# Scores of the first attention pass as float32r products in two halves of the array, with products that nobody reads

## The chip, the core and the metric

The kernel runs on one core of a Trainium2 chip. The metric is the device time of one execution in microseconds. The engines of a core work side by side and wait for each other by semaphores: TensorE (PE in the rows; its weight loads are PEld), VectorE (DVE), ScalarE (ACT), GpSimd (POOL) and SyncE (SP, which issues the transfers here; SPq is its queue).

## What is computed

A vision transformer's layer on 128 images. The part that the change touches is the first attention, without a mask, over 197 tokens of 192 numbers in 12 heads of 16:

```python
x = (tokens - mean) / jnp.sqrt(var + LN_EPS) * ln_w + ln_b
xh = x.reshape(n, SEQ, N_HEADS, D_HEAD)
q = jnp.einsum('bshd,hed->bshe', xh, Wq) + bq[None, None]
k = jnp.einsum('bshd,hed->bshe', xh, Wk) + bk[None, None]
v = jnp.einsum('bshd,hed->bshe', xh, Wv) + bv[None, None]
att = jax.nn.softmax(jnp.einsum('bshd,bthd->bhst', q, k) / jnp.sqrt(jnp.float32(D_HEAD)), axis=-1)
msa = jnp.einsum('bhst,bthd->bshd', att, v).reshape(n, SEQ, HIDDEN_D)
return tokens + msa
```

Behind it come a second attention with a causal mask, a layer norm, a mixture of experts with soft routing, and another layer norm.

## The kernel before, in words

The program is five passes over the images, each with its own tiles and a barrier behind it: `embed_pass` (patches to tokens, norm, q, k and v of the first attention), `attend_pass(causal=False)` (tiles a_...), `attend_pass(causal=True)` (tiles c_...), routing with the experts (r_..., x_...) and `combine_pass` (o_...). Each pass is a pipeline written by hand: in step c, every engine works on several images, each at another stage. `pipeline` (L124) writes the first steps and the last out, and makes the middle a loop of R = 4 steps; in the first attention pass the steps 0 to 7 are written out, and the loop begins with step 8. In the loop an image's number is an expression of the loop's register, and `is_number(i)` (L84) is true only where the number is known when the program is built.

Scores need float32 accuracy. So `embed_pass` splits q and k into three bfloat16 parts: ScalarE the high part (L310), VectorE the remainder `rest` (L338), GpSimd the middle and low parts (L282, L284). SP stores them to `qk1`, three parts of two bytes. The first attention pass loads them stacked: 6 pairs of parts, each of 16 rows, give a contraction of 96 rows (`STACK`) in which one bfloat16 product has all that counts of q times k. Three more rows (`AUG`) carry the negated maxima of the scores in three parts against rows of ones.

One step of the first attention pass has six slots k = 0 to 5 on TensorE (L901 to L972). In each slot stand, for image b4, four key products (`key_scores`, L843, into the banks `sk`; they include the rows of the maxima, and ScalarE's exponential reads them, L713), and for image b2, four query products (`query_scores`, L821, two into each of the banks `sq`; VectorE takes their maxima, L770, which are all that is kept of them). A query product waits until VectorE has read the bank's content before. Then the slot's other work follows: in slot 0 the tokens are turned (L925, float32) and the value products of the last group (L858, float32, four column strips of 32) stand; in slot 1 the maxima are turned (L890) and the sums (L864); in slot 2 the q projection for the second attention (`turned_times`, L873, twelve float32r products) and value products; in slot 3 the sums are turned (L864); in slot 4 the k projection and value products; in slot 5 the v projection (L881, twelve float32r products). Between the q and the k projection ScalarE and VectorE split q (L726, L784). GpSimd splits the maxima (`max_parts`, four operations, L611 to L618), and SP writes their three rows into `qs` (L561).

The routing pass already has `keep_warm` (L1230): products of a tile of ones into a bank that nobody reads, one at three places of a step, and 24 at step 12.

Of the kernel before, what the change touches and what calls it, by code (L numbers as in the profile page):

```python
# [22 lines left out]
F32 = mybir.dt.float32  # L23
# [7 lines left out]
HEADS = 12  # L31
# [150 lines left out]
def embed_pass(nc, n, A, scr):  # L182
    R = 4
    DEPTH = 4
    with ExitStack() as ctx:
# [17 lines left out]
        rest = m.sb("e_rest", [CH, 2, 2, 2, SP])  # L203
        parts = m.sb("e_parts", [CH, R, 2, 2, PARTS, SP], BF16)
# [30 lines left out]
        middle = m.event("e_middle", 2)  # L235
        low = m.event("e_low", 2)
# [5 lines left out]
        def _(sp):  # L242
# [10 lines left out]
            def step(c):  # L253
# [4 lines left out]
                if b.inside(n):  # L258
                    sp.wait_ge(v_copied.sem, v_copied.at(b))
                    for rows in SHARES:  # L260
                        sp.dma_start(scr["tv1"][b.number, rows], tv[rows, b.place]).then_inc(stored.of(b), 16)
                    sp.wait_ge(low.sem, low.at(b))
                    sp.dma_start(scr["qk1"][b.number].rearrange("i c a p s -> p (i c a) s"),
                                 parts[:, b.place].rearrange("p i c a s -> p (i c a) s")).then_inc(stored.of(b), 16)
# [3 lines left out]

        @block.gpsimd
        def _(pool):  # L270
            for e in (middle, low):
                e.seed(pool)

            def step(c):
                b = c - 3
                u = b.parity
                if b.inside(n):
                    for i in range(2):
                        pool.wait_ge(left.sem, left.at(b, i + 1))
                        pool.wait_ge(stored.of(b - 4), stored.at(b - 4))  # L280
                        m.hold(pool)
                        pool.tensor_copy(parts[:, b.place, i, :, place_of(i, 1)], rest[:, u, i]).then_inc(middle.sem, 1)  # L282
                        pool.wait_ge(middle.sem, middle.at(b, i + 1))
                        pool.tensor_tensor(parts[:, b.place, i, :, place_of(i, 2)], rest[:, u, i], parts[:, b.place, i, :, place_of(i, 1)],  # L284
                                           ALU.subtract).then_inc(low.sem, 1)
            pipeline(pool, n, DEPTH, R, step)

        @block.scalar
        def _(act):
# [5 lines left out]
            def step(c):  # L295
# [11 lines left out]
                for i, (done, p) in enumerate(((q_done, qp), (k_done, kp))):  # L307
                    if b3.inside(n):
                        act.wait_ge(done.sem, done.at(b3))
                        split_high(nc.scalar, parts[:, b3.place, i, :, place_of(i, 0)], p[:], SCALES[i]).then_inc(high.sem, 1)  # L310
# [9 lines left out]
        def _(dve):  # L320
# [14 lines left out]
            def left_of(b3, i, p):  # L335
                dve.wait_ge(high.sem, high.at(b3, i + 1))
                dve.wait_ge(low.sem, low.at(b3 - 2, i + 1))
                nc.vector.scalar_tensor_tensor(out=rest[:, b3.parity, i], in0=p[:], scalar=SCALES[i],  # L338
                                               in1=parts[:, b3.place, i, :, place_of(i, 0)], op0=ALU.mult,
# [88 lines left out]
def attend_pass(nc, n, A, scr, causal):  # L428
# [4 lines left out]
    with ExitStack() as ctx:  # L433
        m = Memory(nc, ctx, R)
        qs = m.sb(X + "qs", [AUG, R, HEADS, SP], BF16)
        ks = m.sb(X + "ks", [AUG, R, HEADS, SP], BF16)
# [5 lines left out]
        mxp = m.sb(X + "mxp", [HEADS, 2, PARTS, SP], BF16)  # L442
# [18 lines left out]
        else:  # L461
            rest = m.sb(X + "rest", [CH, 2, SP])
            kf = m.sb(X + "kf", [CH, 2, SP])
# [22 lines left out]
        qk_in_place = m.transfers(X + "qk_in_place", 2 * PARTS)  # L486
# [9 lines left out]
        max_in_place = m.transfers(X + "max_in_place", 3)  # L496
# [33 lines left out]

        def heads_of(fill):
            return (fill % 2, 2 * (fill // 2)) if causal else (fill // 6, 2 * (fill % 6))

        @block.sync
        def _(sp):
# [7 lines left out]
            def step(c):  # L543
                b = c - 1
                if b.inside(n):
                    sp.wait_ge(scored_k.sem, scored_k.at(b - R))
                    at = 0
                    for a in range(PARTS):
                        rows = slice(at, at + (PARTS - a) * DH)
                        at = rows.stop  # L550
                        for i, (stack, of) in enumerate(((qs, slice(0, PARTS - a)), (ks, slice(a, PARTS)))):
# [1103 lines left out]
```

## Time and profile before

| | us |
|---|---|
| median of 3 runs (4807.69 to 4813.0) | 4812.62 |
| the profiled execution | 4837.32 |
| its span, first to last instruction | 4835.4 |

| engine | busy us | share of the span |
|---|---|---|
| TensorE products | 4495.4 | 93% |
| TensorE weight loads | 3885.2 | 80% |
| VectorE | 3048.0 | 63% |
| ScalarE | 2720.1 | 56% |
| GpSimd | 2701.4 | 56% |

The span's stages follow one another, so a share of the whole span tells little of a stage: the stretches have to be read by themselves. A product's recorded duration contains its way through the array; the pace of products is read from start to start. The granted clock of TensorE has two levels in the rows, 1.00 and 0.50 of 2.4 GHz.

### The profile page before, as it was taken

How to read it: one execution, taken by the hardware profiler on the slowest of the kernel's cores; microseconds unless marked ns; L12 is line 12 of the kernel's file. 1: busy time of each engine (PE TensorE's matmuls, PEld its weight loads, DVE VectorE, ACT ScalarE, POOL GpSimd, SP SyncE). 2: the span in 40 equal slices, each digit the busy share in tenths (PEclk: the TensorE clock that was granted, in tenths of full speed). 3: DMA queues.
4: the chain of work that ended last, by engine and by line, in shares of the span. 5: the costliest groups of instructions: out<-in, count | busy, mean ns of one | idle time of the engine just before them, and what ended most of it. 6: DMA issues, size and time to landing. Idle time of an engine off the chain costs nothing. (4 is left out here: it accounts for less than half of the span.)

```text
span 4835.4 us, 161306 instructions
## 1 busy us (share of the span) xinstructions
PE 4495.4 (93%) x48311; PEld 3885.2 (80%) x48311; DVE 3048.0 (63%) x8728; ACT 2720.1 (56%) x6788; POOL 2701.4 (56%) x4491
## 2 busy tenths in 40 slices
PE   8999999899999999999979999999999788889965
PEld 8999999688888888888868888888887566678853
DVE  4555555566666666666647777777776799930058
ACT  3444444466666666666635555555555477753346
POOL 3444444466666666666646666666666588841135
PEclk9999999899999999999979999999999799999965
DMA  6777777677777777777756666666664233369978
GB/s 170 202 202 202 203 202 201 151 166 165 168 168 167 168 166 168 165 165 167 169 110 141 145 142 145 142 146 143 146 141 111 76 93 93 93 156 247 241 233 258
DMA packets 697918, 789.88 MB, mean 163 GB/s; under 512 B 367345, under 2 KB 519887, under 8 KB 697840
## 3 DMA queue, kind: packets, MB, share of 16 engines
q1 hardware_dynamic: 697840, 788.92, 67.6%
q8 instruction: 40, 0.66, 0.1%
q14 instruction: 38, 0.31, 0.0%
HBM read 519.30 MB, written 265.72 MB: 162 GB/s over the span
## 5 line engine op out<-in xcount | busy, mean ns | idle before, releaser
L770 DVE TENSOR_REDUCE a_mx<-a_sq 99x2 f32<-99x394 f32 x1536 | 797.3, 560 | 378.5 <-PE a_sq L821 378.2
L770 DVE TENSOR_REDUCE c_mx<-c_sq 99x2 f32<-99x198 f32 (+1 forms) x1536 | 641.8, 458 | 255.9 <-PE c_sq L821 254.6
L713 ACT ACTIVATE a_ex<-a_sk 99x792 f32<-99x792 f32 (+1 forms) x768 | 638.1, 831 | 107.8 <-PE a_sk L843 57.3
L713 ACT ACTIVATE c_ex<-c_sk 99x792 f32<-99x792 f32 (+1 forms) x768 | 509.4, 663 | 208.2 <-PE c_sk L837 137.7
L379 PE MATMUL e_tokp<-e_wmap,e_ptT 128*99 128x192 f32 x3072 | 544.2, 327 | 20.8 <-DVE e_cvar L332 20.8
L379 PEld LDWEIGHTS e_tokp<-e_wmap,e_ptT 128*99 128x99 f32 x3072 | 483.2, 167 | 21.2 <-issue 20.8
L821 PE MATMUL a_sq<-a_ks,a_qs 96*99 96x198 bf16 x3072 | 441.1, 255 | 31.6 <-DMA a_ks<-scr_qk 16.6
L634 POOL TENSOR_SCALAR_AFFINE_SELECT c_ex<-c_ex 99x396 f32<-99x396 f32 (+1 forms) x768 | 408.0, 546 | 91.5 <-ACT c_ex L713 82.0
L282 POOL CAST e_parts<-e_rest 96x396 bf16<-96x396 f32 x256 | 176.4, 689 | 482.5 <-DVE e_rest L338 482.5
L821 PE MATMUL c_sq<-c_ks,c_qs 96*99 96x99 bf16 (+1 forms) x3072 | 424.8, 231 | 0.0
L843 PE MATMUL a_sk<-a_qs,a_ks 99*99 99x198 bf16 (+1 forms) x3072 | 408.7, 254 | 2.7 <-issue 2.1
L843 PEld LDWEIGHTS a_sk<-a_qs,a_ks 99*99 99x99 bf16 (+1 forms) x3072 | 287.5, 126 | 124.3 <-issue 112.9
L818 PE MATMUL c_sq<-c_maskb,c_identb 99*99 99x198 bf16 x1536 | 366.0, 261 | 20.8 <-DMA c_ks<-scr_qk 17.7
L821 PEld LDWEIGHTS a_sq<-a_ks,a_qs 96*99 96x99 bf16 x3072 | 293.1, 126 | 82.2 <-DVE a_mx L770 46.8
L858 PE MATMUL a_pvp<-a_ex,a_vx 99*32 99x198 f32 (+1 forms) x6144 | 337.9, 337 | 0.6 <-issue 0.5
L821 PEld LDWEIGHTS c_sq<-c_ks,c_qs 96*99 96x99 bf16 x3072 | 319.1, 129 | 0.0
L858 PE MATMUL c_pvp<-c_ex,c_vx 99*32 99x198 f32 (+1 forms) x6144 | 278.6, 299 | 37.7 <-DVE c_on L793 28.1
L858 PEld LDWEIGHTS c_pvp<-c_ex,c_vx 99*32 99x32 f32 (+1 forms) x6144 | 163.3, 110 | 137.8 <-DVE c_on L793 86.9
L698 ACT COPY c_ot<-c_pvp 128x198 f32<-128x198 f32 x384 | 120.9, 315 | 238.8 <-PE c_pvp L858 238.8
L284 POOL TENSOR_TENSOR e_parts<-e_rest,e_parts 96x396 bf16<-96x396 f32 x256 | 225.0, 879 | 20.5
L1359 ACT ACTIVATE x_hid<-x_hp,x_bias 128x128 f32<-128x128 f32 x384 | 119.8, 363 | 207.0 <-PE x_hp L1391 207.0
L818 PEld LDWEIGHTS c_sq<-c_maskb,c_identb 99*99 99x99 bf16 x1536 | 196.7, 128 | 46.0 <-issue 17.9
(196 smaller groups left out, 11575.7 us busy)
## 6 DMA issues: line engine op xcount, KB each, us to landing
e_ptT<-in_x SPq DMA_DIRECT2D x128, 594.0 KB
x_w<-in_fc SPq DMA_DIRECT2D x128, 576.0 KB, 6.6
scr_qk<-e_parts SPq DMA_DIRECT2D x128, 445.5 KB
scr_qk<-a_parts SPq DMA_DIRECT2D x128, 445.5 KB
scr_tv<-e_tv SPq DMA_DIRECT2D x128, 288.0 KB
a_tv<-scr_tv SPq DMA_DIRECT2D x128, 288.0 KB
scr_tv<-a_res SPq DMA_DIRECT2D x128, 288.0 KB
c_tv<-scr_tv SPq DMA_DIRECT2D x128, 288.0 KB
```

The source lines that it names most:

```text
L282: pool.tensor_copy(parts[:, b.place, i, :, place_of(i, 1)], rest[:, u, i]).then_inc(middle.sem, 1)
L284: pool.tensor_tensor(parts[:, b.place, i, :, place_of(i, 2)], rest[:, u, i], parts[:, b.place, i, :, place_of(i, 1)], ALU.subtract).then_i ...
L379: mm = nc.tensor.matmul(tokp[b.parity][:, t], ptT[:, b.place, k, t * TT:(t + 1) * TT], wmap[:, k], start=(k == 0), stop=(k == KC - 1))
L634: pool.affine_select(block_of, block_of, pattern=[[0, G], [1, TT]], compare_op=ALU.is_ge, fill=0.0, base=0, channel_multiplier=-1).then_in ...
L698: nc.scalar.copy(ot[:, b.parity, g], pv).then_inc(o_copied.sem, 1)
L713: nc.scalar.activation(to, of, ACT.Exp).then_inc(exped.sem, 1)
L770: nc.vector.reduce_max(mx[:, b2.parity, qt, h:h + 2], sq[f % 2][:, :, 0:width], AX.X).then_inc(maxed.sem, 1)
L818: nc.tensor.matmul(bank[:, :, qt * TT:(qt + 1) * TT], identb[:], maskb[:].broadcast_to([TT, 2, TT]), start=True, stop=False, skip_group_ch ...
L821: mm = nc.tensor.matmul(bank[:, j, 0:keys], qs[0:STACK, b.place, h + j, qt * TT:(qt + 1) * TT], ks[0:STACK, b.place, h + j, 0:keys], start ...
L843: mm = nc.tensor.matmul(buf[0:rows, a, j * SP:(j + 1) * SP], ks[:, b.place, h, kt * TT:kt * TT + rows], qs[:, b.place, h, :], start=True, ...
L858: mm = nc.tensor.matmul(to, vx[0:rows, b.place, kt, G * g + j, :], of, start=(kt == 0), stop=(kt == 1), skip_group_check=causal)
L1359: a = nc.scalar.activation(hid[:, b.parity, 2 * i + k], hp[i][:, k], ACT.Gelu, bias=bias[:, b.place, 2 * i + k:2 * i + k + 1])
```

## The change

In the embedding pass, q and k are split into two float32r parts instead of three bfloat16 ones: ScalarE writes the high part, VectorE the remainder, rounded, right into `parts`; GpSimd has no work there any more. `qk1` holds two parts of four bytes. The first attention pass keeps heads 0 to 5 in the partitions 0 to 49 and heads 6 to 11 in 64 to 113: three pairs of parts (high x high, high x low, low x high) of 16 rows, 48 in all, and two rows for the maxima. `shared_scores` replaces `key_scores` and `query_scores` there: key and query products alternate, and the heads are ordered so that one stands in the lower half of the rows when the other stands in the upper. Ones for all rows of the maxima are written first, by GpSimd and VectorE, and the first loads wait for them; the loads are eight transfers instead of six, the maxima's rows four instead of three. `max_parts` has two operations instead of four. `keep_warm` puts a product of 512 columns, which nobody reads, ahead of slot 0's turning and of the q and k projections. The second attention pass keeps its bfloat16 scores.

```diff
@@ embed_pass
-        rest = m.sb("e_rest", [CH, 2, 2, 2, SP])
-        parts = m.sb("e_parts", [CH, R, 2, 2, PARTS, SP], BF16)
+        parts = m.sb("e_parts", [CH, R, 2, 2, 2, SP], F32R)
...
-                    sp.wait_ge(low.sem, low.at(b))
+                    sp.wait_ge(left.sem, left.at(b))
...
-        @block.gpsimd
-        def _(pool):
...
-                        pool.tensor_copy(parts[:, b.place, i, :, place_of(i, 1)], rest[:, u, i]).then_inc(middle.sem, 1)
...
-                        pool.tensor_tensor(parts[:, b.place, i, :, place_of(i, 2)], rest[:, u, i], parts[:, b.place, i, :, place_of(i, 1)],
-                                           ALU.subtract).then_inc(low.sem, 1)
...
-                dve.wait_ge(low.sem, low.at(b3 - 2, i + 1))
-                nc.vector.scalar_tensor_tensor(out=rest[:, b3.parity, i], in0=p[:], scalar=SCALES[i],
+                dve.wait_ge(stored.of(b3 - 4), stored.at(b3 - 4))
+                nc.vector.scalar_tensor_tensor(out=parts[:, b3.place, i, :, 1], in0=p[:], scalar=SCALES[i],
...
@@ attend_pass
+            qs = m.sb(X + "qs", [128, R, HC, SP], F32R)
+            ks = m.sb(X + "ks", [128, R, HC, SP], F32R)
...
+            fill = m.sb(X + "fill", [128, 640], BF16)
...
+        def half(h):
+            return slice(64 * (h // HC), 64 * (h // HC) + 3 * DH), slice(64 * (h // HC), 64 * (h // HC) + 3 * DH + 2)
+
         def heads_of(fill):
+            if not causal:
+                return ((0, 6), (1, 6), (0, 8), (1, 8), (0, 10), (0, 0), (1, 10), (1, 0), (0, 2), (1, 2), (0, 4), (1, 4))[fill]
...
+                        if b.is_number(0):
+                            sp.wait_ge(ks_ones, 1)
+                            sp.wait_ge(ks_ones_above, 1)
+                        for c2 in range(2):
+                            for stack, i, at, of in ((qs, 0, 0, slice(0, 1)), (qs, 0, DH, slice(0, 2)),
+                                                     (ks, 1, 0, slice(0, 2)), (ks, 1, 2 * DH, slice(0, 1))):
...
+            if not causal:
+                ones_of_keys(ks[32:64].rearrange("p r h s -> p (r h s)").bitcast(F32))
             pool.memset(vx[:], 0.0).then_inc(zeroed, 1)
...
+                if not causal:
+                    pool.tensor_tensor(low, of, high.bitcast(F32), ALU.subtract).then_inc(max_low.sem, 1)
+                    return
...
+            def shared_scores(b4, b2, k):
+                g, kt = k // 2, k % 2
+                rows = TT - kt
+                if b4.inside(n):
+                    bank_of_keys(b4, k)
+                for j in range(G):
+                    f = 2 * k + j // 2
+                    if b4.inside(n):
+                        h = G * g + j
+                        mm = nc.tensor.matmul(sk[k % 2][0:rows, j // 2, (j % 2) * SP:(j % 2 + 1) * SP],
+                                              ks[half(h)[1], b4.place, h % HC, kt * TT:kt * TT + rows],
+                                              qs[half(h)[1], b4.place, h % HC], start=True, stop=True)
...
+                    if b2.inside(n):
+                        qt, h = heads_of(f)
+                        h += j % 2
+                        if j % 2 == 0:
+                            bank_of_queries(b2, f)
+                        mm = nc.tensor.matmul(sq[f % 2][:, j % 2], qs[half(h)[0], b2.place, h % HC, qt * TT:(qt + 1) * TT],
+                                              ks[half(h)[0], b2.place, h % HC], start=True, stop=True)
...
+            def keep_warm(times):
+                for _ in range(times):
+                    nc.tensor.matmul(work[:], fill[:, 0:128], fill[:, 128:640], start=True, stop=True)
...
+                        shared_scores(b4, b2, k)
...
+                        if not causal:
+                            keep_warm(24 if b6.is_number(2) else 1)
...
+                            keep_warm(1)
                             turned_times(0, q_done)
...
+                        keep_warm(1)
                         turned_times(1, k_done)
@@ scratch
-              "qk1": ([n, 2, 2, PARTS, CH, SP], BF16), "qk2": ([n, 2, 2, PARTS, CH, SP], BF16),
+              "qk1": ([n, 2, 2, 2, CH, SP], F32), "qk2": ([n, 2, 2, PARTS, CH, SP], BF16),
```

The order on TensorE before, in the first slot of the loop of the first attention pass, which is step 8 (sk are the banks of the key scores, sq0 and sq1 those of the query scores; ISA and REGISTER_ALU rows prepare waits):

```order
L131 ISA
L904 ISA
L906 REGISTER_ALU
L832 ISA
L843 MATMUL a_sk0<-a_qs,a_ks 99x198 x4
L813 ISA
L821 MATMUL a_sq0<-a_ks,a_qs 99x198 x2
L813 REGISTER_ALU
L821 MATMUL a_sq1<-a_ks,a_qs 99x198 x2
L920 REGISTER_ALU
L921 REGISTER_ALU
L925 MATMUL a_work<-a_ident,a_res 96x99 x4
```

The same place after the change, from the second key product on (L886 are the key products, L896 the query products, L949 the product that nobody reads, L993 the turning of the tokens):

```order
L886 MATMUL a_sk0<-a_qs,a_ks 99x198
L896 MATMUL a_sq0<-a_ks,a_qs 99x198
L886 MATMUL a_sk0<-a_qs,a_ks 99x198
L836 REGISTER_ALU
L896 MATMUL a_sq1<-a_ks,a_qs 99x198
L886 MATMUL a_sk0<-a_qs,a_ks 99x198
L896 MATMUL a_sq1<-a_ks,a_qs 99x198
L983 REGISTER_ALU
L984 REGISTER_ALU
L949 MATMUL a_work<-a_fill 128x512
L993 MATMUL a_work<-a_ident,a_res 96x99 x4
L1013 ISA
```

Key and query products alternate, the wait for the second query bank has moved between them, and one L949 stands ahead of the turning. It is one here too, in the step whose image b6 is number 2; no other step of this pass has more than one at that place.

In the routing pass, whose first 16 steps are written out, the place with 24 reads, after the change as before it but for the line numbers (L1349 are the logits, L1313 and L1320 turn them and the tokens):

```order
L1349 MATMUL r_lgp<-r_slotsT,r_xnT 99x64 x4
L1303 MATMUL r_unread<-r_fill 128x512 x24
L1313 MATMUL r_lgT<-r_ident,r_lg 64x99 x2
L1320 MATMUL r_xtp<-r_ident,r_xn 96x99 x4
L1303 MATMUL r_unread<-r_fill 128x512
```

Nothing moved there; it is the only row of 24 such products in the program.

## Rows read from the trace of the kernel before

**Rows 1.** Busy by stretch: us, busy (x instructions) of PE PEld DVE ACT POOL, clock, DMA.

```profile
200.00:800.00 600.00, 600.00 (x4433) 596.40 (x4432) 321.07 (x710) 264.69 (x796) 273.34 (x355) 1.00 0.76 202
1100.00:1700.00 600.00, 594.99 (x7241) 500.20 (x7240) 411.05 (x904) 398.08 (x704) 366.12 (x602) 1.00 0.74 167
4640.00:4835.00 195.00, 102.61 (x512) 64.47 (x512) 161.04 (x704) 118.89 (x256) 100.65 (x128) 0.50 0.83 261
```

**Rows 2.** Timeline of TensorE, first attention pass, one step: start, us, engine, line, operation.

```profile
1499.79 0.55 PE L843 MATMUL a_sk<-a_qs,a_ks 99*98 99x198 bf16 x4
...
1502.05 0.34 PE L873 MATMUL a_work<-a_hTh,a_wl 96*96 96x198 f32 x2
...
1502.79 0.35 PE L873 MATMUL a_work<-a_hTl,a_wh 96*96 96x198 f32 x2
...
1503.88 0.55 PE L843 MATMUL a_sk<-a_qs,a_ks 99*98 99x198 bf16 x4
...
1504.62 0.49 PE L864 MATMUL a_pvp<-a_ident,a_ot 128*99 128x128 f32 x3
...
1505.30 0.82 PE L821 MATMUL a_sq<-a_ks,a_qs 96*99 96x198 bf16 x4
...
1508.36 0.51 PE L821 MATMUL a_sq<-a_ks,a_qs 96*99 96x198 bf16 x4
...
1509.78 0.51 PE L843 MATMUL a_sk<-a_qs,a_ks 99*99 99x198 bf16 x4
...
1510.48 0.50 PE L925 MATMUL a_work<-a_ident,a_res 99*96 99x99 f32 x4
...
1511.73 0.55 PE L843 MATMUL a_sk<-a_qs,a_ks 99*98 99x198 bf16 x4
```

**Rows 3.** Timeline of TensorE in the last pass, and in the embedding pass.

```profile
4702.55 1.60 PE L1557 MATMUL o_zp<-o_yb,o_mix 64*99 64x192 f32 x8 [1.38 <-POOL o_yb L1487]
...
303.40 2.12 PE L379 MATMUL e_tokp<-e_wmap,e_ptT 128*99 128x192 f32 x12
```

**Rows 4.** Timeline of TensorE's products and loads in the routing pass, 4054.3 to 4056.

```profile
4054.40 0.33 PE L1268 MATMUL r_cTp<-r_ident,r_cw 99*64 99x99 f32 x2
4054.66 0.38 PE L1271 MATMUL r_dTp<-r_ident,r_dw 64*99 64x64 f32 x2
4054.98 0.39 PE L1233 MATMUL r_unread<-r_fill 128*128 128x512 bf16 x1
4055.21 0.83 PE L1279 MATMUL r_lgp<-r_slotsT,r_xnT 96*99 96x64 f32 x8
...
4054.66 0.25 PEld L1271 LDWEIGHTS r_dTp<-r_ident,r_dw 64*99 64x99 f32 x2
```

**Rows 5.** Timeline of VectorE, first attention pass; in brackets its idle time before.

```profile
1503.85 0.57 DVE L784 SCALAR_TENSOR_TENSOR a_rest<-a_work,a_parts 96x396 f32<-96x396 f32 x1 [0.77 <-ACT a_parts L179]
1504.64 1.04 DVE L770 TENSOR_REDUCE a_mx<-a_sq 99x2 f32<-99x394 f32 x2 [0.22 <-PE a_sq L821]
```

**Rows 6.** DMA issues: out<-in, engine, count, size.

```profile
scr_qk<-e_parts SPq DMA_DIRECT2D x128, 445.5 KB
```

**Rows 7.** Timeline of all engines at the start of the first attention pass.

```profile
904.86 2.66 POOL L596 MEMSET a_vx<- 99x3072 f32 x1 [6.69 <-issue]
...
905.29 0.42 SPq L552 DMA_DIRECT2D a_qs<-scr_qk  x1
...
907.89 4.06 POOL L600 MEMSET a_ks<- 3x4752 f32 x1
```

**Rows 8.** Busy by stretch, as rows 1: around the clock's rise, and routing's start.

```profile
915.00:933.70 18.70, 14.98 (x68) 9.07 (x69) 15.60 (x28) 3.65 (x6) 2.97 (x7) 0.50 0.75 143
933.70:960.00 26.30, 24.79 (x302) 18.84 (x301) 18.86 (x42) 17.44 (x29) 9.46 (x18) 1.00 0.57 121
...
3777.00:3811.00 34.00, 30.47 (x138) 22.09 (x139) 25.44 (x126) 17.51 (x81) 20.39 (x31) 0.50 0.25 76
```

More of the change, by code:

```diff
@@ L485, in attend_pass @@
         ks_ones = m.sem(X + "ks_ones")
-        qk_in_place = m.transfers(X + "qk_in_place", 2 * PARTS)
+        filled = m.sem(X + "filled")
+        ks_ones_above = m.sem(X + "ks_ones_above")
+        qk_in_place = m.transfers(X + "qk_in_place", 2 * PARTS if causal else 8)
         tv_in_place = m.transfers(X + "tv_in_place", 2)
@@ L495, in attend_pass @@
         max_low = m.event(X + "max_low")
-        max_in_place = m.transfers(X + "max_in_place", 3)
+        max_in_place = m.transfers(X + "max_in_place", 3 if causal else 4)
         v_spread = m.event(X + "v_spread")
@@ L559, in step @@
                     sp.wait_ge(max_low.sem, max_low.at(b))
-                    for a in range(PARTS):
-                        sp.dma_start(qs[STACK + a:STACK + a + 1, b.place], mxp[:, b.parity, a]).then_inc(max_in_place.of(b), 16)
+                    if causal:
+                        for a in range(PARTS):
+                            sp.dma_start(qs[STACK + a:STACK + a + 1, b.place], mxp[:, b.parity, a]).then_inc(max_in_place.of(b), 16)
+                    else:
+                        for a in range(2):
+                            for c2 in range(2):
+                                at = 64 * c2 + 3 * DH + a
+                                sp.dma_start(qs[at:at + 1, b.place].bitcast(F32),
+                                             mxp[c2 * HC:(c2 + 1) * HC, b.parity, a].bitcast(F32)).then_inc(max_in_place.of(b), 16)
                 b = c - 2
@@ L605, in max_parts @@
             def max_parts(b):
-                high, mid, low = (mxp[:, b.parity, a] for a in range(PARTS))
+                high, mid, low = (mxp[:, b.parity, a] for a in range(PARTS)) if causal else (mxp[:, b.parity, a] for a in (0, 0, 1))
                 of, left = mxn[:, b.parity], mxr[:, b.parity]
@@ L830, in key_scores @@
                 buf = sk[k % 2]
-                if k < 2:
-                    pe.wait_ge(exped.sem, exped.at(b - 1, 5 + k))
-                else:
-                    pe.wait_ge(exped.sem, exped.at(b, k - 1))
-                if causal and kt:
+                bank_of_keys(b, k)
+                if kt:
                     for j in range(G):
@@ L896, in step @@
                     pe.wait_ge(ks_ones, 1)
+                    if not causal:
+                        pe.wait_ge(ks_ones_above, 1)
                     pe.wait_ge(vx_ones, 1)
@@ L906, in step @@
                         pe.wait_ge(qk_in_place.of(b2), qk_in_place.at(b2))
-                    if b4.inside(n):
-                        key_scores(b4, k)
-                    if b2.inside(n):
-                        query_scores(b2, 2 * k)
-                        query_scores(b2, 2 * k + 1)
+                    if causal:
+                        if b4.inside(n):
+                            key_scores(b4, k)
+                        if b2.inside(n):
+                            query_scores(b2, 2 * k)
+                            query_scores(b2, 2 * k + 1)
+                    else:
+                        shared_scores(b4, b2, k)
                     if k == 0 and b6.inside(n):
```

100 lines of the change are left out of this document (58 added, 42 removed).

## The prediction

> **What bounds the kernel now.** Read the busy times by stretch first: they tell which engine a stage waits for. In the embedding pass (200 to 800) TensorE is busy 600 of 600 us and DMA has a share of 0.76; in the first attention pass (1100 to 1700) TensorE is busy 595 of 600 while VectorE has 411, ScalarE 398 and GpSimd 366 [rows 1]. So both passes that the change touches are TensorE's, and what counts is the length of TensorE's own list of work in one step. The step is read from TensorE's timeline: the same row comes back after 1511.73 - 1499.79 = 11.94 us [rows 2], and about 120 steps are full. The sum is made against the profiled execution (4837.32 us, span 4835.4), 0.5% above the median of the runs; the differences are put on the median, 4812.62. About 0.2% (9.6 us) is what a measurement can tell.
>
> **The scores before.** Each of six slots has eight score products. From the first (1509.78) to the next work (1510.48) is 0.70 us; behind the value products, whose arrangement of the array is another, it is 0.74 (1503.88 to 1504.62) [rows 2]. Three of each: 4.32 us.
>
> **The scores after.** The same 48 products of 198 columns, but a key product (rows 0 to 63 or 64 to 127) and a query product in the other half stand behind each other, and write other PSUM banks. Do two halves run at once? The last pass has the only such products of this trace: eight instructions of 64 rows and 192 columns in 1.60 us at a granted clock of 0.50, while twelve of 128 rows and 192 columns take 2.12 at 1.00, 0.16 each, which is 0.32 at half the clock; eight of those would need 2.6 [rows 1, 3]. So they go in pairs, and their loads too. What float32r costs is in the projections: eight products of 198 columns from 1502.05 to 1502.79, 0.0925 each [rows 2]. I take 0.0925 for a pair: 4 x 0.0925 = 0.37 a slot. The bounds are 0.0825 (what is left of the 0.0925 if the halves smooth each other, an estimate) and 2 x 0.0925 (float32r in halves is not in the trace, only float32).
>
> **What comes with it: switches.** The score products now use the array in halves, everything else in the step uses it whole or in column strips. The routing pass shows such a change: after two products of 99 rows begun at 4054.40 (0.33 for both, the last of a row alone 0.25, so 0.08 apart), the array is through at about 4054.57; the first of 64 rows loads at 4054.66 [rows 4]. That is 0.09 us of nothing, and the weight load behind it isn't hidden: float32 products of 64 columns with 99 columns of weights come at 0.083 (eight in 0.83), a pace set by the load; I take 0.085. The way back costs the same 0.09: the second of the two can't stream before its own load, so by these paces it ends near 4054.88 (an estimate), and 4054.98 is the next load [rows 4]. Bounds: 0, if other waits cover a switch, and 0.12. The step had 6 switches, in and out of the value products three times. Now every slot goes whole, halves, whole or strips: 15, so 9 more.
>
> The Trainium skill ("TensorEngine Tiling (Array Packing)", Theoretical Speedup) gives products of 64 rows or fewer up to twice the rate; by that alone the scores would take 2.16 us and the step would change by -2.16 + 0.69 = -1.47, not by the +0.08 below. The same page (Key Properties) says that changing the mode, not the tile, drains the engine, without a price; the rows charge 0.09 for it.
>
> **The sum of a full step.** Scores 6 x (0.085 + 0.37) = 2.73 instead of 4.32: -1.59. Nine switches: +0.81. Two loads of about 99 float32 columns that were hidden behind scores and now stand behind a switch (turning the sums in slot 3, the v projection in slot 5): +0.17. Three unread products of 512 columns, 4054.98 to 4055.21 with a short load: 3 x 0.23 = +0.69 [rows 4]. Together **+0.08 us**.
>
> The waits: in slot 4 the queries stand 0.82 instead of 0.51, 0.31 lost to VectorE's maxima [rows 2]. That chain runs from the q projection over ScalarE to VectorE's remainder (1503.85) and two maxima from 1504.64, the first of which waits 0.22 for TensorE [rows 5]. After the change the list between the q projection and that point is shorter by about 0.28, and the first maximum can begin 0.30 earlier: the wait stays near 0.25, -0.06. So +0.02 a step, 120 x 0.02 = **+3 us**. The 0.01 of the pair's pace is 24 x 0.01 = 0.24 us a step, 29 us in all, and is the main width of the forecast.
>
> **What is free.** The embedding pass loses four GpSimd operations an image and VectorE's wait for them; TensorE, busy 600 of 600, covers it. Its store of q and k grows from 445.5 KB [rows 6] by a third, from six bytes an element to eight: 148.5 KB more for each of 128 images, 19.5 MB in the pass's some 870 us, 22 GB/s on top of 202, and the last pass moves 261 [rows 1]. In the attention pass GpSimd loses two of four operations on the maxima, with 234 of 600 us idle already. The loads of q and k move the same bytes in pieces twice as long; SP issues 17 instead of 14 transfers a step, at 0.43 each 7.3 of 11.94 us [rows 7]. If DMA were late, TensorE would stand at the first score of a step.
>
> **The start of the pass.** The first loads now wait for GpSimd's ones in the keys, which come first there: 4.06 us from 904.86, so 908.9 instead of 905.29, and there are two more transfers ahead of the first score: **+4.5 us** [rows 7]. The clock matters more. It was granted at 0.50 (1.2 GHz) until 933.7, then at 1.00 (2.4 GHz), when key scores had joined the queries' [rows 8]. The new scores leave gaps at that place. The 24 unread products that might raise it are **not in the built program**: they hang on image 2 at step 8, and the loop begins at step 8, where the image's number is unknown when the program is built; the order shows one L949 there, and x24 only in the routing pass. At half the clock a step is longer by what streams: 12 less 15 x 0.09 of switches, 0.25 of waits and some 0.7 of exposed loads, 9.5 us. I take two full steps, **+19 us**, because projections, an unread product and value products then follow each other with one switch; the bounds are 0 (it rises as early as before) and all 120 steps (a rival).
>
> Forecast: 3 + 4.5 + 19 = 26, **4839 us**.
>
> **The rivals.**
> - *The halving comes through, faster.* The nine switches and exposed loads are hidden or not charged: 0.08 - 0.81 - 0.17 - 6 x 0.085 = -1.41 us a step, of which VectorE's chain takes some 0.2 back; 120 x -1.2 = -145, so about 4690. For it: the waits for maxima could cover a switch. Against it: the wait stands inside the scores, not at their edge, and the routing pass pays both ways with nothing else to wait for [rows 4]. It decides for faster where a switch costs under 0.06. The Trainium skill's rule of the double rate, quoted above, would by itself lead here, and the pairs [rows 3] agree with the rate.
> - *float32r in halves doesn't pair.* Then a slot's scores are 0.085 + 8 x 0.0925: +2.22 us a step, +266, less the waits it fills (30): 5075. For it: the pair seen is float32, at half the clock. Against: all else of it is alike.
> - *The clock stays at 0.50.* +9.5 x 120 less the waits: about 5930. For it: in the routing pass three unread products a step did not raise it from 3777 to 3811 [rows 8], and the 24 are missing here. Against: that pass has short products and many waits, and the clock here rose before without any unread product.
>
> **How the numbers follow.** Forecast case 0.62 (its own range 4800 to 4890: pair at 0.0825 or 0.10, no cold step to five); halving 0.16; no pairs 0.09; cold clock 0.13. Of the forecast case 0.13 falls under -0.2%, 0.13 within 0.2%, 0.36 above. Faster 0.13 + 0.16 = 0.29; same 0.13; slower 0.36 + 0.09 + 0.13 = 0.58. The range 4690 to 5000 takes in the forecast case, the nearer part of the halving and a clock that comes up only after up to 17 steps; no pairs and the long cold clock are left out.
>
> **What would show it.** In the profile after: key and query products starting in twos, 0.09 apart; idle of 0.09 before and behind each slot's scores; a step of 11.9 to 12.0; the clock at 0.50 until about 980 to 1000. A step under 11.2 would make the switches wrong, one over 13.5 the pairs, a clock of 0.50 far into the pass the start.

## The result, and the profile after

| | before | changed |
|---|---|---|
| median of the runs, us | 4810.15 (4800.39 to 4813.0) | 4884.18 (4852.18 to 4927.41) |
| ratio to before, 95% interval | | 1.0135 (1.0097 to 1.0174) |
| profiled execution, us (span) | 4837.32 (4835.4) | 4927.41 (4925.7) |
| first score product of the attention pass, us | 913.2 | 916.8 |
| a full step at a granted clock of 1.00, us | 11.94 | 12.16 |
| a full step at 0.50, us | none | 20.37 |

The change is slower by 1.35%. Its profiled execution is the longest of its four, and the ratio is made without it. First the stretches of the changed kernel, to be read against [rows 1] and [rows 8] (us, then busy us and instructions of PE, PEld, DVE, ACT and POOL, granted clock, DMA share, GB/s):

```profile
200.00:800.00 600.00, 600.00 (x4432) 596.33 (x4431) 272.23 (x710) 264.63 (x796) 0.00 (x0) 1.00 0.78 224
...
919.00:1148.00 229.00, 221.11 (x1588) 160.56 (x1606) 107.53 (x223) 90.11 (x153) 64.44 (x102) 0.50 0.45 100
1149.00:2400.00 1251.00, 1232.26 (x14919) 939.59 (x15126) 838.10 (x1850) 823.50 (x1440) 669.42 (x1026) 1.00 0.80 164
...
1300.00:1900.00 600.00, 590.88 (x7161) 450.63 (x7252) 401.64 (x887) 395.19 (x691) 321.43 (x493) 1.00 0.80 164
```

The embedding pass is as it was: TensorE busy 600 of 600, GpSimd empty, 224 GB/s instead of 202; its last product starts at 896.2 before and at 896.3 after. The attention pass has a long stretch at a clock of 0.50 that before lacks: until 1148.6, where before rose at 933.7 [rows 8]. The length of a step shows in the transposes at its head, which come back once a step; first at 0.50, then at 1.00:

```profile
1040.10 0.86 PE L993 MATMUL a_work<-a_ident,a_res 99*96 99x99 f32 x4 [0.34 <-issue]
1060.46 0.86 PE L993 MATMUL a_work<-a_ident,a_res 99*96 99x99 f32 x4 [0.33 <-issue]
...
1570.35 0.51 PE L993 MATMUL a_work<-a_ident,a_res 99*96 99x99 f32 x4 [0.16 <-issue]
1582.52 0.51 PE L993 MATMUL a_work<-a_ident,a_res 99*96 99x99 f32 x4 [0.16 <-issue]
```

So 20.36 and 12.17. The pass, from its first score to its last product, takes 1663.6 us in the profiled execution instead of 1553.3, 110 more. Its first 14 steps (counted by VectorE's first maximum of a step) take 239.0 instead of 155.0: 84 more. The next 112 take 1362.3 instead of 1337.4: 25 more. Between the routing pass and the last pass, which the change does not touch, the profiled execution of before was 30 us longer (353 against 323; the experiments have 320 to 332, and one 341); that is why the two spans differ by 90 and not by some 120.

Over the runs the same parts give: 119 steps x 0.22 = 26, 3.6 for the start, and of the 65 to 70 us some 35 to 40 are left for the slow first steps. A step at 0.50 costs 20.37 - 12.16 = 8.2 us, so that would be four or five of them, where the profiled execution has nine and a part.

The mean granted clock of each run bears this out. It is 0.938 in the profiled execution and 0.947, 0.949 and 0.957 in the others, with spans of 4925.7, 4888.3, 4876.6 and 4850.5, which makes 611, 518, 497 and 417 us at 0.50 (twice what the mean lacks to 1.00, times the span). The others thus had 93, 113 and 194 us less of it, the length of 4.6, 5.6 and 9.5 slow steps, and were 37, 49 and 75 us shorter: about 8 us for each such step. So two of them had some four or five slow steps and the fastest next to none. The mean clock of before's runs varies from 0.956 to 0.963 by itself, so a count can be off by a step or two.

Inside a step at 1.00, slots 3 and 4 on TensorE (start, us, line, operation):

```profile
1563.61 0.33 PE L886 MATMUL a_sk<-a_qs,a_ks 50*98 50x198 f32 x1
1563.61 0.33 PE L896 MATMUL a_sq<-a_ks,a_qs 48*99 48x198 f32 x1
1563.78 0.26 PE L886 MATMUL a_sk<-a_qs,a_ks 50*98 50x198 f32 x1
...
1563.96 0.25 PE L896 MATMUL a_sq<-a_ks,a_qs 48*99 48x198 f32 x1
1564.15 0.57 PE L917 MATMUL a_pvp<-a_ident,a_ot 128*99 128x128 f32 x3
1564.65 0.33 PE L886 MATMUL a_sk<-a_qs,a_ks 50*99 50x198 f32 x1
1564.70 0.33 PE L896 MATMUL a_sq<-a_ks,a_qs 48*99 48x198 f32 x1
...
1564.92 0.25 PE L886 MATMUL a_sk<-a_qs,a_ks 50*99 50x198 f32 x1
1565.17 0.33 PE L896 MATMUL a_sq<-a_ks,a_qs 48*99 48x198 f32 x1
...
1565.57 0.54 PE L926 MATMUL a_work<-a_hTh,a_wh 96*96 96x198 f32 x2
```

Slot 3 is what the prediction drew: a key and a query product start together, the first pair takes 0.17 (one load stands in the open), the next ones 0.09 each, and 0.19 after the last pair's start, 0.0925 of streaming and 0.09 of nothing, the transposes start: 0.54 in all. Slot 4 takes 0.92: at 1564.92 the products stop for 0.25. VectorE at that time:

```profile
1563.49 0.57 DVE L810 SCALAR_TENSOR_TENSOR a_rest<-a_work,a_parts 96x396 f32<-96x396 f32 x1 [1.06 <-ACT a_parts L179]
1564.08 1.04 DVE L796 TENSOR_REDUCE a_mx<-a_sq 99x2 f32<-99x394 f32 x2
1565.04 0.22 DVE L817 RECIPROCAL a_rec<-a_pvp 99x12 f32<-99x12 f32 x1
```

Its two maxima of slot 3 stand from 1564.08 to 1565.12; the query product at 1565.17 needs the bank that the second of them empties. From its first score to its last, slot 4 takes 0.70 where slot 3 takes 0.36, so 0.33 is lost, the load that stands in the open behind the stop included. Before lost 0.31 in slot 4 [rows 2, 5] and 0.12 in slot 2, whose query products take 0.63 instead of 0.51:

```profile
1501.40 0.63 PE L821 MATMUL a_sq<-a_ks,a_qs 96*99 96x198 bf16 x4
```

Read the same way, on the mean from 1300 to 1900, the change loses 0.06, 0.17 and 0.33 in slots 1, 2 and 4: 0.56 against 0.43. The first score of slot 4 comes 1.04 after that of slot 3 (1563.61 to 1564.65), while the maxima of slot 3 end 1.51 after it. They cannot begin before its products are through, and VectorE's list is as long as it was.

### The profile page after: what moved, and what is told of

The parts are those of the page before. It is cut to its first block and busy times, and to the rows that moved or that the text cites. A ratio compares the mean times of both kernels' runs of the same rounds, so it can differ in the third digit from the quotient of the medians.

```text
span 4925.7 us, 160854 instructions
## 1 busy us (share of the span) xinstructions
PE 4573.2 (93%) x48376; PEld 3844.4 (78%) x48695; DVE 2984.1 (61%) x8730; ACT 2730.8 (55%) x6788; POOL 2205.1 (45%) x3723
## 5 line engine op out<-in xcount | busy, mean ns | idle before, releaser
L896 PE MATMUL a_sq<-a_ks,a_qs 48*99 48x198 f32 x3072 | 548.3, 292 | 24.4 <-DMA a_ks<-scr_qk 20.1
L886 PE MATMUL a_sk<-a_qs,a_ks 50*99 50x198 f32 (+1 forms) x3072 | 532.9, 289 | 1.1 <-issue 1.1
L886 PEld LDWEIGHTS a_sk<-a_qs,a_ks 50*99 50x99 f32 (+1 forms) x3072 | 367.3, 171 | 184.9 <-issue 134.9
L896 PEld LDWEIGHTS a_sq<-a_ks,a_qs 48*99 48x99 f32 x3072 | 371.8, 172 | 52.9 <-DVE a_mx L796 27.9
L911 PE MATMUL a_pvp<-a_ex,a_vx 99*32 99x198 f32 (+1 forms) x6144 | 360.1, 355 | 0.0
L926 PE MATMUL a_work<-a_hTh,a_wh 96*96 96x198 f32 x1024 | 236.9, 314 | 0.0
L911 PEld LDWEIGHTS a_pvp<-a_ex,a_vx 99*32 99x32 f32 (+1 forms) x6144 | 166.8, 114 | 83.5 <-issue 6.7
```

What stands on the lines that cost most here:

```text
L886: mm = nc.tensor.matmul(sk[k % 2][0:rows, j // 2, (j % 2) * SP:(j % 2 + 1) * SP], ks[half(h)[1], b4.place, h % HC, kt * TT:kt * TT + rows] ...
L896: mm = nc.tensor.matmul(sq[f % 2][:, j % 2], qs[half(h)[0], b2.place, h % HC, qt * TT:(qt + 1) * TT], ks[half(h)[0], b2.place, h % HC], st ...
L911: mm = nc.tensor.matmul(to, vx[0:rows, b.place, kt, G * g + j, :], of, start=(kt == 0), stop=(kt == 1), skip_group_check=causal)
L926: mm = nc.tensor.matmul(onT[:, o], of, by, start=(j == 0), stop=(j == len(pairs) - 1))
```

## Experiments on the clock

**The 24 where they take effect.** The condition is moved from image 2, which falls into the loop, to image 1, in the last step that is written out.

```diff
-                            keep_warm(24 if b6.is_number(2) else 1)
+                            keep_warm(24 if b6.is_number(1) else 1)
```

> The change with its 24 unread products placed in step 7, the last step that is written out, so that they are in the program. In the change's profile the attention pass ran ten steps of 20.37 us at a granted clock of 0.50 before its steps came to 12.16. Theory: it is the missing 24 that leave the clock low; with them it is at 1.00 by step 9, so the time is 4810 + 120 x 0.22 + 4 + some 10 = 4840 to 4855, and repeats agree within 15 us instead of the 75 of the change. Rival: 24 products do not lift it, or it falls again behind them: 4850 to 4930 as the change, with the same spread.

Measured: 4855.52 us (4842.52 to 4871.43), 1.0106 (1.0074 to 1.0138) of before. In its profile one full step at 0.50 is left (20.51), the next takes 18.23, and all behind it 12.16. The theory holds in mechanism, and the median lies at the end of its range; repeats still differ by 29 us, not 15. The change is then 50 us above the before of its time: 25 from the steps, 3.6 from the start, and 22 that the first 14 steps are longer.

**The change once more, unaltered.**

> The changed kernel once more, unaltered. Theory: its step is 20.37 at a granted clock of 0.50 and 12.16 at 1.00 as in its first profile, and only the number of steps at 0.50 is another, since the times of its repeats differ by 75 us: span less 8.2 us for each step that it has fewer. Rival: the difference between repeats lies elsewhere in the program, and the number of slow steps is ten again.

Measured: 4917.25 us, span 4915.5, 10.2 below the first. The step is 20.36 and 12.16 again, and one step fewer stands at 0.50 (eight of full length instead of nine). The number of slow steps does differ. The runs down to 4852 have no profile; for them the mean clocks above speak.

**No unread product at all.** The three calls are taken out.

> The change without any unread product in the attention pass. Theory: each of the three costs its 0.23 us on TensorE's own list, so a step at full clock is 12.16 - 0.69 = 11.47, below the 11.94 of before; what the clock does at the start is open, as long as it rises within some 20 steps the time is 4760 to 4830. First rival: the unread products hold the clock, without them it stays at 0.50 for most of the pass: 5300 to 5850. Second rival: they stand in waits for other engines and cost next to nothing: the step stays at 12.0 to 12.2.

Measured: 5757.13 us (5752.54 to 5783.34), 1.1999 (1.1964 to 1.2034). The first rival holds. The page's row of the granted clock, in tenths by 40 slices of the span, and the stretch of the pass:

```profile
PEclk9999996555555555555555559999999989999985
```

```profile
960.00:3400.00 2440.00, 2439.81 (x18067) 1801.93 (x18065) 1055.55 (x2238) 1016.13 (x1760) 817.74 (x1255) 0.50 0.43 101
```

TensorE is busy 2439.81 of 2440 us, and the clock is not raised before the pass is over; a step takes 19.41.

**Only the 24.** The burst stays, and the loop has no unread product.

```diff
-                            keep_warm(24 if b6.is_number(2) else 1)
+                            keep_warm(24 if b6.is_number(1) else 0)
...
-                            keep_warm(1)
                             turned_times(0, q_done)
...
-                        keep_warm(1)
```

> The 24 unread products in step 7 and none in any other step. Theory: the clock is up from step 9 on and stays up, since before had no unread products at all; step 11.47, time 4810 - 120 x 0.47 + 4 + 10 = 4768, faster than both kernels. Rival: without the three a step the clock falls again in the pass, with stretches at 0.50: each step there costs 8 us more, so 4850 and above.

Measured: 4805.28 us (4794.25 to 4817.49), 0.9994 (0.9979 to 1.0008): no difference from before that can be measured. The clock, once up, stays up:

```profile
1000.00:2400.00 1400.00, 1378.12 (x17138) 1044.71 (x17135) 961.52 (x2142) 954.40 (x1666) 778.15 (x1191) 1.00 0.78 170
```

This is the same loop as in the run before, instruction for instruction: started at 0.50 it stays there, started at 1.00 it stays there too. The three unread products a step are therefore what brings the changed kernel up at all, late and at no fixed step; with 24 in a row the clock is up while they run (they begin at 974.8, and it rises at 977.0), and the three are then needless. My time of 4768 was wrong by 37. The step is 11.77 on the mean, not 11.47, for two reasons. An unread product takes 0.23 of TensorE's list (slot 0: 0.77 with one, 0.55 without), but a weight load that would stand in the open is hidden by it: without it the first two products of the q projection take 0.27 and not 0.185 (second pair of lines below). From a slot's last score to its value products, slots 2 and 4 are 0.15 shorter without, slot 0 0.19, together 0.48 and not 0.69. And without them TensorE arrives earlier at places where it waits (first pair), which costs the other 0.09:

```profile
1500.46 0.25 PE L896 MATMUL a_sq<-a_ks,a_qs 48*99 48x198 f32 x1
1500.86 0.33 PE L943 MATMUL a_work<-a_ident,a_mx 99*12 99x99 f32 x2 [0.15 <-DVE a_hTl L801]
...
1502.07 0.43 PE L926 MATMUL a_work<-a_hTh,a_wh 96*96 96x198 f32 x2
1502.34 0.35 PE L926 MATMUL a_work<-a_hTh,a_wl 96*96 96x198 f32 x2
```

And the first 14 steps are still 17 us longer than before's, where I had put 10.

## Experiments on the score products

These runs, and the one with shorter maxima, have the 24 where they take effect.

**Both products in one half.** The query products of a slot take heads whose rows lie in the half that the slot's key products use.

```diff
-                return ((0, 6), (1, 6), (0, 8), (1, 8), (0, 10), (0, 0), (1, 10), (1, 0), (0, 2), (1, 2), (0, 4), (1, 4))[fill]
+                return ((0, 0), (1, 0), (0, 2), (1, 2), (0, 4), (0, 6), (1, 4), (1, 6), (0, 8), (1, 8), (0, 10), (1, 10))[fill]
```

> The burst kernel with the query products given other heads in each slot, so that a key product and the query product behind it use the same half of the rows (the same 48 products, the same banks). Theory: two halves ran side by side in the change, now they follow each other, so each slot has 8 x 0.0925 instead of 4 x 0.0925: 6 x 0.37 = 2.2 us more a step, of which the waits for VectorE in slots 2 and 4 (some 0.5) take back a part: a step of 13.9 to 14.4 at full clock. Rival: the records only look paired and the halves share the time: the step stays within 0.2 of 12.16.

Measured: 5039.6 us, a step of 13.45. Slot 1, and behind it slot 3:

```profile
1502.38 0.33 PE L886 MATMUL a_sk<-a_qs,a_ks 50*98 50x198 f32 x1
1502.56 0.25 PE L896 MATMUL a_sq<-a_ks,a_qs 48*99 48x198 f32 x1
1502.65 0.25 PE L886 MATMUL a_sk<-a_qs,a_ks 50*98 50x198 f32 x1
...
1503.12 0.25 PE L896 MATMUL a_sq<-a_ks,a_qs 48*99 48x198 f32 x1
1503.30 0.34 PE L943 MATMUL a_work<-a_ident,a_mx 99*12 99x99 f32 x2
...
1506.83 0.34 PE L886 MATMUL a_sk<-a_qs,a_ks 50*98 50x198 f32 x2
1507.00 0.27 PE L896 MATMUL a_sq<-a_ks,a_qs 48*99 48x198 f32 x2
1507.09 0.27 PE L886 MATMUL a_sk<-a_qs,a_ks 50*98 50x198 f32 x2
1507.19 0.27 PE L896 MATMUL a_sq<-a_ks,a_qs 48*99 48x198 f32 x2
1507.39 0.57 PE L917 MATMUL a_pvp<-a_ident,a_ot 128*99 128x128 f32 x3
```

In slot 1 the eight start 0.09 apart, one after the other: 0.92 until the next work, 0.38 more than a paired slot's 0.54. That is four times 0.0925, so a pair is worth exactly the product that it hides, and the rival falls. The step is below my 13.9 because only four of the six slots did what the edit meant. In slots 2 and 3 the heads 4 to 7 lie in both halves, four products in the lower and then four in the upper, and these ran in twos all the same (slot 3 above: 0.56).

**No halves.** The contraction is over all 128 rows, with the rows between the stacks set to zero. The scores sum two heads, so they are not the reference's, and exponentials and maxima are scaled to stay finite.

```diff
-            return slice(64 * (h // HC), 64 * (h // HC) + 3 * DH), slice(64 * (h // HC), 64 * (h // HC) + 3 * DH + 2)
+            return slice(0, 128), slice(0, 128)
```

> The burst kernel with each score product over all 128 rows (the rows of another head are summed in, and the exponentials and maxima are scaled to keep the numbers finite, so the scores are not those of the reference): float32r as in the change, the same count and columns, but no halves. Against the run with both products in one half this takes away nine switches a step and the exposed weight load behind each switch, and nothing else. Theory: a slot's scores are 8 x 0.0925 = 0.74 with loads hidden: a step is 11.94 + 48 x 0.0045 + 3 x 0.23, less waits that these fill: 12.5 to 12.85, and 1.0 to 1.5 below the run with one half. Rival: a switch costs nothing: both have the same step.

Measured: 4931.72 us, a step of 12.84. Slot 5 and the v projection, then the next step's first score:

```profile
1513.87 0.33 PE L891 MATMUL a_sk<-a_qs,a_ks 128*98 128x198 f32 x1
...
1514.61 0.25 PE L901 MATMUL a_sq<-a_ks,a_qs 128*99 128x198 f32 x1
1514.70 0.35 PE L939 MATMUL a_pvp<-a_wh,a_hTh 96*99 96x192 f32 x2
...
1515.78 0.26 PE L891 MATMUL a_sk<-a_qs,a_ks 128*99 128x198 f32 x1
```

The last score starts at 1514.61 and the projection 0.09 later, with no gap; with halves it was 0.19. From the first score of slot 5 to the next step's first score the run takes 1.90 us; the run with both products in one half takes 2.17 for the same, on the mean of the steps from 1300 to 1900. Of the 0.27, 0.09 is the way out of the halves, 0.08 the projection's load, which now stands in the open (its first two products take 0.26 instead of 0.18), and 0.09 the way back. The load of the first score behind the way back costs another 0.08 (0.17 instead of 0.09 to the second score), which this stretch leaves out. Slot 1 with what stands behind it gives 0.28. The rival falls: switches are paid at every slot, at the 0.09 of [rows 4]. The step is only 0.62 below that of the run with both products in one half, where I had 1.0 to 1.5, because two slots of that run went in twos.

This run's clock also differs. Its first unread product starts at 959.5, and the clock is up before it, from 945.1:

```profile
919.00:945.00 26.00, 19.65 (x92) 14.86 (x92) 17.76 (x32) 4.31 (x6) 2.82 (x6) 0.50 0.82 153
945.20:959.00 13.80, 13.13 (x148) 10.40 (x149) 10.13 (x22) 9.18 (x15) 2.46 (x4) 1.00 0.44 103
```

The run with both products in one half has as many products of as many columns, and unread ones from 960.2 on, and is at 0.50 until 985.9.

## Experiments on the waits

**Shorter maxima.** VectorE looks at the first 99 of the 198 scores of each row; the maxima of the others are left out.

```diff
-                            width = (TT if qt == 0 else SP) if causal else SEQ
+                            width = (TT if qt == 0 else SP) if causal else TT
```

> The burst kernel with VectorE's maxima over the first 99 of the 198 scores of a row (the maxima of the others are left out), so that each of the twelve takes about half. Theory: in the change the score products of slots 2 and 4 last 0.72 and 0.92 us against 0.55 in slots 3 and 5, because the query products wait for VectorE to empty a bank; with short maxima these waits go: step 12.16 - 0.17 - 0.37 = 11.6. Rival: they wait for ScalarE's exponentials or for something else: step stays within 0.1 of 12.16.

Measured: 4793.44 us, a step of 11.67 on the mean against 12.16. Slot 2 falls from 0.71 to 0.55, slot 4 from 0.92 to 0.59. The waits are VectorE's, half a microsecond in each step.

**The remainder later.** The q remainder, which waits for ScalarE, moves behind slot 3's maxima (on top of the early kernel, told last).

```diff
-                        if k == 2 and not causal:
+                        if k == 3 and not causal:
                             dve.wait_ge(q_high.sem, q_high.at(b6))
```

> The early kernel with VectorE's remainder of q moved in its list from behind the maxima of slot 2 to behind those of slot 3. Theory: the wait in slot 4 is VectorE being late because its remainder stands ahead of slot 3's maxima and waits there for ScalarE; with the remainder behind them the first of them starts 0.5 us earlier, slot 4's score products fall from some 0.88 to 0.55, and the step from 11.75 to 11.42: 4792 - 120 x 0.33 = 4752. Rival: the remainder is then late for the k projection in slot 4, which needs its bank empty: the wait moves there and the step stays within 0.1.

Measured: 4802.61 us (4788.34 to 4822.72), 0.9988 (0.9973 to 1.0003), 10 above the early kernel instead of 40 below. The step grows from 11.76 to 11.87 and slot 4 from 0.88 to 1.00. VectorE there:

```profile
1508.31 1.04 DVE L797 TENSOR_REDUCE a_mx<-a_sq 99x2 f32<-99x394 f32 x2 [1.49 <-PE a_sq L901]
1509.27 0.56 DVE L811 SCALAR_TENSOR_TENSOR a_rest<-a_work,a_parts 96x396 f32<-96x396 f32 x1
```

The maxima now begin as soon as slot 3's products are through, after VectorE has stood idle for 1.49, and yet slot 4 loses what it lost: 0.69 from its first score to its last, 0.70 in the early kernel. Its third query product waits for the second maximum, which ends at 1509.36. And the remainder ends at 1509.83, later than TensorE wants to begin the k projection that needs its bank:

```profile
1509.16 0.25 PE L891 MATMUL a_sk<-a_qs,a_ks 50*99 50x198 f32 x1
1509.41 0.33 PE L901 MATMUL a_sq<-a_ks,a_qs 48*99 48x198 f32 x1
...
1509.88 0.42 PE L931 MATMUL a_work<-a_hTh,a_wh 96*96 96x198 f32 x2
```

So the theory fails at its first step, since the remainder was not what made the maxima late, and the rival is right about what is added: 0.12 ahead of the k projection.

**The turned maxima later as well.** In slot 1 the sums are turned first.

```diff
-                    if k == 1 and b3.inside(n) and not causal:
-                        turn_maxima(b3, b6)
...
                         turn_sums(b5, 0)
+                    if k == 1 and b3.inside(n) and not causal:
+                        turn_maxima(b3, b6)
```

> The kernel before this one, and in slot 1 the turning of the sums ahead of the turning of the maxima, which waits for VectorE's hTl. Theory: 0.15 of a step was TensorE standing there; the three turns of the sums fill it: step 11.42 - 0.1 to 0.15, 12 to 18 us less in all. Rival: the turned maxima come 0.35 later, and ScalarE's copy and the stores of the maxima with them, or slot 1 only hands the wait on to the next slot's query products: no change or slower.

Measured: 4806.44 us (4799.02 to 4813.8), 0.9994 (0.9985 to 1.0004); step 11.88. Slot 1's scores fall from 0.79 to 0.55 and slot 2's rise from 0.60 to 0.79: handed on, as the rival has it.

**The remainder later, in the kernel before.**

> The kernel before the change with only that move of VectorE's remainder. It tells how much of that gain needs the change. Theory: slot 4 of before waits 0.26 for VectorE by the same mechanism, so its step falls from 11.94 to about 11.7, 4810 - 30 = 4780, and the changed kernel with the move stays some 25 us faster. Rival: before's scores take longer, so its VectorE is less late and the move brings under 10 us.

Measured: 4852.16 us (4848.01 to 4858.52), 1.0089 (1.0072 to 1.0106): slower by 45, where theory and rival both had a gain. Its slot 4 grows from 0.95 to 1.27, the step from 11.94 to 12.28. The scores themselves take as long as before (0.92 from first to last); all that is added stands between the last score and the k projection, 0.35 instead of 0.03. Before's scores take 0.2 longer in a slot, so the maxima come later and the remainder behind them later still. The order that the kernel had was right, and the wait is not an order but VectorE's length of list between the q and the k projection.

## The version that beats both

The burst goes to where TensorE has nothing to do, ahead of the first score; two unread products stand in most slots of the steps written out, none in the loop; and of the first loads only the two into rows with ones wait for these.

```diff
+                pe.wait_ge(filled, 1)
+                for _ in range(24):
+                    nc.tensor.matmul(work[:], fill[:, 0:128], fill[:, 128:640], start=True, stop=True)
...
                         shared_scores(b4, b2, k)
+                        if b2.is_number(0):
+                            keep_warm(2)
+                        for i in (1, 2, 3):
+                            if b2.is_number(i) and k in (0, 3, 4, 5):
...
+                                keep_warm(2)
```

> No unread product in the loop of the pass; 24 of them ahead of the pass's first score, while TensorE waits for the first loads, and two in most slots of the steps that are written out; and of the first loads only the two that write into rows which the ones were put into wait for them. Theory: the clock is up before the first full step, which saves the two steps of 19.55 and 18.03 us that the run with only the burst had (14 us less some 3 for the products themselves), and the loads come 2 to 3 us earlier: 4805 - 13 = 4792, 0.3% under before. Rival: the clock falls again in the steps with scores alone, since TensorE waits for VectorE there, and comes up no earlier or not at all: 4805 or more, up to 5750.

Measured: 4792.24 us (4786.02 to 4799.66), 0.9963 (0.9946 to 0.998) of before: faster by 0.37%. TensorE ahead of the pass, and four stretches:

```profile
902.70 8.08 PE L837 MATMUL a_work<-a_fill 128*128 128x512 bf16 x24 [9.55 <-DMA a_ident<-in_ident]
910.71 0.61 PE L901 MATMUL a_sq<-a_ks,a_qs 48*99 48x198 f32 x4
```

```profile
902.70:908.30 5.60, 5.60 (x14) 1.97 (x15) 3.67 (x1) 0.00 (x0) 5.10 (x3) 0.50 0.65 150
908.60:921.80 13.20, 12.74 (x65) 6.13 (x62) 9.38 (x18) 1.42 (x2) 1.34 (x3) 1.00 0.93 194
922.50:942.00 19.50, 19.42 (x114) 9.16 (x112) 11.59 (x21) 6.31 (x10) 1.87 (x4) 0.50 0.41 94
...
960.00:2400.00 1440.00, 1418.05 (x17634) 1074.12 (x17632) 988.34 (x2200) 979.83 (x1714) 797.94 (x1224) 1.00 0.75 169
```

The clock is up during the 24 already, falls once more for 20 us while the pipeline fills, and is at 1.00 from 942.4 on, ahead of the first full step. The first 14 steps take 5 us more than before's instead of 17, and each later step 0.18 less. The rival was half right, a second stretch at 0.50 came, and it decided nothing.

## Why the prediction was right, and where it was not

The direction and the range hold; the size was 26 us and is 65 to 70. Part of that was luck: 23 of the 26 us were the start and the cold clock, and the 26 us that the step costs were put at 3.

- **The scores, right.** A pair at 0.0925, taken from the pair in float32 [rows 3] and the projections [rows 2], is what the trace shows, and the rival that float32r in halves does not pair is gone by the run in one half. What the Trainium skill ("TensorEngine Tiling (Array Packing)", Theoretical Speedup) states, up to twice the rate, is met for the products; the step estimated from it alone, 1.47 shorter, is not, for the next reason.
- **The switches and exposed loads, right.** The forecast without waits was +0.08. The changed step less its waits is 12.16 - 0.56 = 11.60, before's 11.94 - 0.43 = 11.51: +0.09. The run with short maxima, 11.67 with the 0.06 of slot 1 still in it, gives 11.61. The rival in which the halving comes through needed a switch under 0.06; the run over all rows has 0.09 each way, and 0.08 for a load behind it.
- **The unread products, right as a term of this sum** (0.23 each), in which they hide the loads of what follows them. As a price it is too high: taken out, they give back 0.39 a step of 0.69.
- **The waits, wrong.** "The wait stays near 0.25, -0.06" is the step that failed at full clock. The forecast looked at slot 4 alone, where the loss went from 0.31 to 0.33, and not at slots 1 and 2, where it went from 0.12 to 0.23. That is +0.13 instead of -0.06, and accounts for the step: 0.09 + 0.13 = +0.22. I had worked out when VectorE could begin its maxima, and not that a slot of 0.54 hands it the next two maxima before it is through with the last.
- **The embedding pass and the transfers, right.** 202 + 22 = 224 GB/s was worked out, and 224 is in the row; TensorE stays at 600 of 600.
- **The start, right in size:** 3.6 instead of 4.5.
- **The cold clock: right that it would come, wrong in the reason and too small.** "Two full steps" was taken because products follow each other more closely there, and the rise in before "without any unread product" was held against the rival. The run without unread products shows that this loop does not rise by itself in 2400 us. It is the three products that lift it, after a number of steps that differs between runs: between next to none and five by the mean clocks, eight and nine by the profiles. The step's price at 0.50 is 8.2, not 9.5 (the terms named there add up to 9.7). Of the difference 0.5 are waits, which vanish there (slots 1 to 5 take 0.92 to 0.97 each); where the rest lies no run shows. That the 24 are missing from the program was read rightly. In the profiles the first 14 steps fall from 239.0 and 230.8 to 176.6 with them, but over the runs the ratio goes from 1.0135 to 1.0106, some 14 us, which the intervals do not separate.

What is open: what in the loop's list of work keeps the clock at the level where it finds it, and why the three unread products lift it once after nine steps and once after fewer. The runs narrow the first. Without any unread product the clock rose in the three kernels whose scores do not stand in halves (before at 933.7, before with the later remainder at 948.1, the run over all rows at 945.1), and in no kernel with halves did it rise ahead of one. Whether it is the halves, the switches or, in part, the pairs is not separated; the run with both products in one half, where four of six slots have no pairs, stayed low as well. Nor is it known whether before always rises: two of its 17 runs beside the last version, left out of the ratio there, took 5067 and 5074 us at a mean granted clock of 0.89, some 700 us more at 0.50 than the others, and in which pass is not on record.

## What to carry to other kernels

A product that gets twice as fast gives to the step only what is left after the switches around it and after the engine that empties its banks; count both for each place where the work stands, not for the work. A list that holds the full clock may be unable to reach it, so look at what the clock is when a loop is entered, and raise it in a stretch where the engine idles rather than pay for it in every step. And look in the built program whether a one-time instruction is there: a condition on a number that only the loop knows leaves it out silently.

## What was not expected of the hardware

- The same loop ran 2440 us at 0.50 with TensorE busy throughout, and 1400 us at 1.00 with TensorE busy 98% of the time; only the first steps differed.
- The two halves do not need their products in turn. With four products of the lower half ahead of four of the upper in the program, the first of each started 0.013 us apart (two L886 at 1506.83, then two L896 at 1507.00), and the slot took 0.56, as with the products in turn; with all eight in one half a slot took 0.92.
- Of the three unread products a step, the trace of the change has a record of one only (49 in the 600 us from 1300), while that of the run in one half has all three (134 in as long). Their weight loads are all in the trace of the change (148), so a gap marked "issue" ahead of the transposes there is such a product, not idle time.
